# Four-layer recurrent network on one core: head sums of layer 1 go to TensorE, row scalings of the mixer to ScalarE, and the order of all steps is laid out anew

## The reference, cut to what matters

```
# layer 1, for each token: q, k, v are 16 heads of 8
z[h, g]   = sum over d of q[h, d] * k[g, d]          # 16 x 16 scores
w         = entmax15(z)                               # over g
s[h, d]   = sum over g of w[h, g] * v[g, d]
# layer 0, for each chunk: state kept per head
xdt       = x * dt                  # per token and head
xdd       = xdt * decay             # per token and head
state     = state * exp(A_sum) + B^T xdd
```

## Time and profile before

| | us |
|---|---|
| median of 3 runs | 3212.22 (3211.52 to 3215.06) |
| span of the profiled execution, first to last instruction | 3209.0 |
| what lies around the span (median less span) | 3.2 |
| layers 0, 1 and first half of 2, from the span's start | 1945 |
| second half of layer 2 | 288 |
| preparation of layer 3 | 72 |
| attention of layer 3 | 813 |
| feed-forward of layer 3 | 91 |

### The profile page before, as it was taken

How to read it: one execution, slowest core, us unless ns; L and a number is a source line. 1 busy time by engine, 2 the same in 40 slices (tenths; PEclk the granted TensorE clock), 3 DMA queues, 4 the chain that set the end, 5 groups by cost and what they waited for, 6 DMA issues and landing times.

```text
span 3209.0 us, 40003 instructions
## 1 busy us (share of the span) xinstructions
PE 2383.4 (74%) x13729; PEld 1300.2 (41%) x13729; DVE 2544.2 (79%) x5554; ACT 1633.2 (51%) x3182; POOL 565.8 (18%) x610
## 2 busy tenths in 40 slices
PE   3697876967958769679674304997688898888888
PEld 1333333333333333334331101332366676666663
DVE  3386898998999999989989673887577777777764
ACT  1344436245344353353442412666587888777862
POOL 0000300302203003012030020001332323323320
PEclk9698987977978879779777655999799999999999
DMA  2001100100101001001010004200688877888751
GB/s 73 1 22 43 30 25 28 35 32 23 34 29 30 26 24 33 28 27 31 30 24 23 23 8 123 57 9 31 198 226 223 235 222 225 220 215 227 220 157 43
DMA packets 270758, 265.92 MB, mean 83 GB/s; under 512 B 15224, under 2 KB 244235, under 8 KB 268987
## 3 DMA queue, kind: packets, MB, share of 16 engines
q1 hardware_dynamic: 270554, 263.37, 28.8%
HBM read 130.48 MB, written 124.45 MB: 79 GB/s over the span
## 4 chain that ended last, share of the span: by engine, by line
DVE 41%; PE 31%; ACT 14%; issue 9%; DMA 2%; POOL 2%; SPq 1%; DVEq 0%; POOLq 0%; ACTq 0%
PE banks L2642 5%; PE banks L2688 4%; DVE t L2618 3%; DVE t L1017 2%; PE banks L2602 2%; DVE t L1169 2%; ACT L144 2%; DVE t L952 1%; ACT t L2629 1%; PE banks L1085 1%; ACT t L2553 1%; DVE t L2673 1%; DVE t L1700 1%; DVE t L1704 1%; ACT t L1395 1%
## 5 line engine op out<-in xcount | busy, mean ns | idle before, releaser
L2618 DVE CUSTOM_DVE_ANT_0 t<-banks,t 128x640 f32<-128x640 f32 (+7 forms) x512 | 377.8, 747 | 135.2 <-PE banks L2642 62.2
L2629 ACT ACTIVATE t<-t 128x640 f32<-128x640 f32 (+7 forms) x512 | 391.0, 780 | 81.3 <-DVE t L2618 80.4
L2642 PE MATMUL banks<-ident,t 128*128 128x128 f32 x2304 | 360.1, 281 | 41.6 <-DVE t L2839 14.4
L2642 PEld LDWEIGHTS banks<-ident,t 128*128 128x128 f32 x2304 | 253.8, 142 | 108.1 <-ACT t L2629 50.5
L2602 PE MATMUL banks<-t 128*128 128x512 bf16 (+3 forms) x768 | 197.3, 333 | 39.4 <-DVE t L2618 37.5
L2583 POOL TENSOR_TENSOR t<-t 128x512 f32<-128x512 f32 x96 | 122.6, 1277 | 551.1 <-DMA t<-relative_scratch 455.7
L548 POOL TENSOR_TENSOR t<-t 128x512 f32<-128x512 f32 x28 | 48.1, 1718 | 915.7 <-ACT t L520 915.7
L2673 DVE COPY t<-banks 128x512 f32<-128x512 f32 x256 | 175.6, 686 | 32.2 <-PE banks L2642 31.3
L1085 PE MATMUL banks<-t 128*128 128x512 f32 x256 | 145.0, 650 | 42.9 <-DVE t L1165 32.3
L1740 ACT ACTIVATE t<-t 128x16 f32<-128x16 f32 x256 | 82.5, 322 | 184.1 <-DVE t L1704 142.4
L1119 ACT ACTIVATE t<-banks 128x512 f32<-128x512 f32 x128 | 76.4, 597 | 195.6 <-PE banks L1085 195.4
(11 more groups left out here) (453 smaller groups left out, 5956.2 us busy)
## 6 DMA issues: line engine op xcount, KB each, us to landing
relative_scratch<-t SPq DMA_DIRECT2D x128, 512.0 KB, 3.6
t<-relative_scratch SPq DMA_DIRECT2D x128, 512.0 KB, 5.2
relative_scratch<-t SPq DMA_DIRECT2D x128, 256.0 KB, 4.1
t<-in_wmoe SPq DMA_DIRECT2D x64, 384.0 KB, 3.0
t<-cut_scratch SPq DMA_DIRECT2D x192, 64.0 KB
t<-t SPq DMA_DIRECT2D x16, 512.0 KB, 4.2
cut_scratch<-t SPq DMA_DIRECT2D x8, 768.0 KB, 4.1
z_scratch<-t SPq DMA_DIRECT2D x8, 512.0 KB, 3.1
```

What stands on the lines that cost most here:

```text
L2618: nc.vector.tensor_tensor_reduce(s.s[z][:, 0:n], ps[:, b0:b0 + 1 + i // 4, :].rearrange("p b n -> p (b n)")[:, 0:n], s.bias[r][:, j, WIDE ...
L2629: nc.scalar.activation(s.s[z][:, 0:n], s.s[z][:, 0:n], ACT.Exp, scale=-1.0, bias=s.least[:, z:z + 1]).then_inc(*a.mark("weights", u))
L2642: nc.tensor.transpose(ps[:, 4 + c % 2, (t - lo) * P:(t - lo + 1) * P], s.s[u % NS][:, t * P:(t + 1) * P], k.ident[:]).then_inc(*e.mark("tu ...
```

## The change

What it does, part by part:

1. **Scores of att1.** The product (line 952) is laid out as d, h, g in place of h, g, d. The reduction (955) goes; instead TensorE adds the 8 slices of 256 columns into a PSUM bank by 8 matmuls with the identity as weights, and ScalarE copies the sum to `z`.
2. **Output of att1.** The product (1017) is laid out as g, h, d. The reduction (1020) and the transposes (897) go; TensorE adds the 16 slices of 128 columns by 16 matmuls with the slice as weights and the identity as moving data, which also turns the result.
3. **Buffers and banks.** `prod` has two buffers now, the second on the memory of `cum` and `cumsq`. The heads part holds banks 3 and 4 until `z` of the last tile is copied (before: until q, k, v of the last tile are copied).
4. **Mixer.** `xdt`, `xdd` and the scaled state (`kept`, a new buffer) are made by ScalarE, 4 activations with a scale for each row or head; VectorE's lines 599, 611 and 621 go.
5. **Table loads** are issued ahead of the wait of their step in place of behind it.
6. **Order.** All strings `TURNS_*`, `TURNS3_*` and `TURNS4_*` are new.
7. The weights of layer 1 are laid out to match (k by d, v by g), and the masks with them.

```diff
 def att1_pe(k, s, u, free):
...
     for t in range(NT):
-        yield
-        for line, *key in free("heads_out", u):
-            pe.wait_ge(line, *key)
-        pe.wait_ge(v, "s_tok", u, t)
-        nc.tensor.transpose(ps[:, bk, t * P:(t + 1) * P], o.s_tok[:, t], k.ident[:]).then_inc(*e.mark("s_tok", u))
+        for d in range(HD):
+            if d % SOME == 0:
+                yield
+                pe.wait_ge(v, "products", u, t)
...
+            mm(bank(ps, bk + (t + 1) % 2, NH * NH), k.ident[:], o.prod[t % 2][:, d * NH * NH:(d + 1) * NH * NH], start=(d == 0),
+               stop=(d == HD - 1)).then_inc(*e.mark("z", u, t))
+    for t in range(NT):
+        for g in range(NH):
+            if g % SOME == 0:
...
+                pe.wait_ge(v, "valued", u, t)
+            mm(ps[:, bk, t * P:(t + 1) * P], o.prod[t % 2][:, g * D:(g + 1) * D], k.ident[:], start=(g == 0), stop=(g == NH - 1)).then_inc(
+                *e.mark("s_T", u, t))
 def att1_act(k, s, u):
...
+    for t in range(NT):
+        yield
+        act.wait_ge(e, "z", u, t)
+        nc.scalar.copy(o.z[:, t], bank(ps, bk + (t + 1) % 2, NH * NH)).then_inc(*a.mark("z", u, t))
 def att1_dve(k, s, u):
...
-        tt(prod.rearrange("p (h g d) -> p h g d", h=NH, g=NH), rep(q, 2, NH), rep(kk, 1, NH), ALU.mult).then_inc(*v.mark())
-        yield
-        dve.wait_ge(v)
-        reduce(o.z[:, t], prod.rearrange("p (x d) -> p x d", d=HD), AX, ALU.add).then_inc(*v.mark())
+        if t >= 2:
+            dve.wait_ge(e, "z", u, t - 2)
...
+        tt(o.prod[t % 2].rearrange("p (d h g) -> p d h g", h=NH, g=NH), rep(q, 3, NH), rep(kk, 2, NH), ALU.mult).then_inc(
+            *v.mark("products", u, t))
...
-        tt(prod.rearrange("p (h d g) -> p h d g", h=NH, d=HD), rep(w, 2, HD), rep(x, 1, NH), ALU.mult).then_inc(*v.mark())
-        yield
-        dve.wait_ge(v)
-        reduce(o.s_tok[:, t], prod.rearrange("p (x g) -> p x g", g=NH), AX, ALU.add).then_inc(*v.mark("s_tok", u, t))
+        if t >= 2:
+            dve.wait_ge(e, "s_T", u, t - 2)
+        tt(o.prod[t % 2].rearrange("p (g h d) -> p g h d", g=NH, h=NH), rep(w, 3, HD), rep(x, 2, NH), ALU.mult).then_inc(
+            *v.mark("valued", u, t))
 def mixer_act(k, s, u):
...
-        act.wait_ge(v, "xdt", u, t)
+        act.wait_ge(e, "turned", u, t)
         nc.scalar.copy(s.btok[:], ps[:, 0, DI0:DI0 + P]).then_inc(*a.mark("btok", u, t))
+        yield
+        for h in range(H0):
+            nc.scalar.activation(s.xdt[:, h, :], ps[:, 0, h * HP:(h + 1) * HP], ACT.Copy, scale=s.dt[:, t, h:h + 1]).then_inc(
+                *a.mark("xdt", u, t))
...
+        act.wait_ge(a)
+        for h in range(H0):
+            nc.scalar.activation(s.xdd[:, h, :], s.xdt[:, h, :], ACT.Copy, scale=s.dd[:, h:h + 1]).then_inc(*a.mark("xdd", u, t))
+        if u:
+            yield
+            if t:
+                act.wait_ge(v, "state", u, t - 1)
+            for h in range(H0):
+                nc.scalar.activation(s.kept[:, h, :], s.state[:, t, h, :], ACT.Copy, scale=s.ec[:, h, P - 1:P]).then_inc(
+                    *a.mark("kept", u, t))
```

More of the change, by code:

```diff
@@ L513, in mixer_act @@
         yield
+        k.table(LOGEXP)
         act.wait_ge(a)
-        k.table(LOGEXP)
         nc.scalar.activation(s.ec, bank(ps, 2).rearrange("p (h t) -> p h t", h=H0), ACT.Exp).then_inc(*a.mark())
@@ L731, in ffn0_act @@
         yield
+        k.table(SILU)
         act.wait_ge(e, "gate", u, t)
-        k.table(SILU)
         nc.scalar.activation(f.hid[t // 2][:, t % 2], ps[:, S0, 0:FF0], ACT.Silu).then_inc(*a.mark("silu", u, t))
@@ L865, in att1_views @@
     o.qkv = take((NT, 3 * D))
-    o.z, o.cum, o.cumsq = (take((NT, NH * NH)) for _ in range(3))
-    o.s_tok, o.masked = (o.cum.rearrange("p t g -> p (t g)")[:, 0:TB].rearrange("p (t d) -> p t d", t=NT) for _ in range(2))
-    o.prod = take((2 * NT * NH * NH,))
-    o.sa, o.sb = (o.prod[:, i * NT * NH * NH:(i + 1) * NT * NH * NH].rearrange("p (t g) -> p t g", t=NT) for i in range(2))
+    o.z, sums = take((NT, NH * NH)), take((2 * NT * NH * NH,))
+    o.cum, o.cumsq = (sums[:, i * NT * NH * NH:(i + 1) * NT * NH * NH].rearrange("p (t g) -> p t g", t=NT) for i in range(2))
+    o.masked = o.cum.rearrange("p t g -> p (t g)")[:, 0:TB].rearrange("p (t d) -> p t d", t=NT)
+    o.prod = [take((2 * NT * NH * NH,)), sums[:, 0:2 * NT * NH * NH]]
+    o.sa, o.sb = (o.prod[0][:, i * NT * NH * NH:(i + 1) * NT * NH * NH].rearrange("p (t g) -> p t g", t=NT) for i in range(2))
     o.one, o.star, o.tau = take((NT * NH,)), take((NT * NH,)), o.sb
     return o
+SOME = 4
 def att1_pe(k, s, u, free):
@@ L1896, in final @@
 def final(k, name, u):
-    return {"ffn0": (k.line("ffn0_act"), "gate", u), "heads": (k.line("att1_act"), "qkv", u, NT - 1),
+    return {"ffn0": (k.line("ffn0_act"), "gate", u), "heads": (k.line("att1_act"), "z", u, NT - 1),
             "heads_out": (k.line("att1_act"), "s_T", u), "in2": (k.line("in2_act"), "copied", u, NT - 1),
@@ L2153, in readout2_act @@
     yield
+    k.table(ROOT)
     act.wait_ge(e, "var", b)
-    k.table(ROOT)
     nc.scalar.activation(s.stat[:, 0], ps[:, 1, 0:2], ACT.Sqrt, bias=k.eps5[:]).then_inc(*a.mark("root", b))
@@ L2274, in moe2_act @@
     yield
+    k.table(SIGMOID)
     act.wait_ge(e, "logits", b)
-    k.table(SIGMOID)
     nc.scalar.activation(o.rb.score, ps[:, bb, 0:NT * E2].rearrange("p (t e) -> p t e", t=NT), ACT.Sigmoid).then_inc(
@@ L2742 @@
+    "svvstststsvvtsststsvsvtststsvvttssstvstvsststsvvtstsstvsvtsststsvvtsststsvvstststsvvtsststssvvtststvsvttssstsstv"
+    "svtstvsvtstsstsstvstvststvvssttvvvv"
 )
```

304 lines of the change are left out of this document (151 added, 153 removed).

## The result

The changed kernel takes **3208.58 us** (median of 15 runs, 3195.41 to 3215.14) against 3214.45 us of the kernel before on the same chip (15 runs, 3209.22 to 3233.25). The ratio is 0.9964, with an interval from 0.9951 to 0.9977: times 3214, faster by 12 us (7 to 16). The two medians alone lie 6 us apart; wherever a gain is given here, it is worked out from the ratio. The forecast was 158 us. The sign was right, and so was nearly every count of work; the size was not.

What follows compares the result with a forecast made beforehand. VectorE was taken to bound the first stage: 172 us off it less 28 lost gives 144, plus 8 for loads and 6 for later order makes 158, so 3054 us against 3212.22. Range 2995 to 3095 us, chance 0.62.

Steps and rivals of the forecast that it cites:

- The step that failed: First stage: work taken from VectorE shortens the 215.1 us period almost one for one, by 21.5 to 193.6 us.
- Off VectorE: First stage: two reductions a tile (140.8 us) and lines 599, 611, 621 (10.9, 10.9, 9.5) leave VectorE, 172 us.
- the wait for GpSimd: Line 611, mixer: its wait of 1.07 us in 28 cases (30 us) was counted as staying, on the next product.
- The new layout of the two large products: Products of 2048 elements on VectorE: new order costed at nothing, bounds nothing and 22 us.
- TensorE: First stage: sums add 27 us a unit at 2.4 GHz, some 54 at 1.2 GHz; 166 us if the clock is granted.
- ScalarE: First stage: activations, copies and table loads bring it to 113 us a unit, below the period, no term in the sum.
- Table loads: ScalarE: 49 more loads, 127 up to the stage's end; hiding them ahead of waits gives 8 us, between nothing and 45.
- Later stages: After the first stage: the new order of steps gives 6 us, bounds -20 and +30.
- Bank 3 and TensorE take over in part: First stage: rival where the chain of banks 3 and 4 sets about 205 us, gain 80 us, 3132 us; chance 0.17.
- The slower rival: First stage: rival where the hand-over of bank 3 sets the period, 222 us, 56 us more, 3268 us; chance 0.04.
- the signs listed for a wrong forecast: VectorE idle over 25 us a period, TensorE's clock still 0.83, or later stages shorter or longer by over 20 us.

Runs made afterwards that it cites:

- e1: Kernel before, both reductions of layer 1's attention (L955, L1020) reading only the first addend of each sum: 3173.77 us against 3213.48, ratio 0.9887.
- e12: Changed kernel with the old order of the steps after the first stage: 3221.67 us against 3216.85 of the kernel before, ratio 1.0016.
- e2: Kernel before with only the changed order of the later stages (six strings): 3203.93 us against 3213.48, ratio 0.9969.
- e14: Kernel before, both reductions cut to their first addend and the mixer's row scalings on ScalarE, old order: 3193.19 us against 3211.81, ratio 0.994.
- e13: Changed kernel with one sum matmul in place of each group of 8 or 16: 3190.57 us against 3211.81 of the kernel before, ratio 0.9937.
- e3: Kernel before with only the mixer's row scalings moved to ScalarE, in the old order: 3254.23 us against 3213.48, ratio 1.013.
- e8: Changed kernel with the mixer's row scalings put back on VectorE, changed order: 3225.72 us against 3216.49 of the kernel before, ratio 1.0034.
- e7: Kernel before with only ScalarE's table loads moved ahead of their step's waits: 3212.34 us against 3216.49, ratio 0.9987.
- e11: Kernel before with the changed order of the later stages and table loads ahead of their waits: 3188.04 us against 3216.85, ratio 0.9911.
- e10: Changed kernel with each of TensorE's sum matmuls issued twice: 3399.02 us against 3216.85 of the kernel before, ratio 1.0569.
- e6: Kernel before with only the reduction of the output's products (L1020) cut to its first addend: 3208.57 us, ratio 0.9975.
- e5: Kernel before with only the reduction of the scores' products (L955) cut to its first addend: 3205.3 us against 3216.49, ratio 0.9975.
- e15: Changed kernel with one matmul per sum and the mixer's row scalings back on VectorE: 3217.15 us against 3211.81 of the kernel before, ratio 1.002.

## Why the prediction was wrong

**The step that failed** is the one on which the whole sum stood: "Work taken from VectorE here should shorten the period almost one for one", and so "215.1 - 21.5 = 193.6 us". The runs show 36 us back for 115 removed, with nothing added elsewhere (e1). Two readings led to it. A busy share of 94% was taken for a bound. And small waits were taken to confirm it: "with a bank chain as the bound they would have to be far larger". They need not be. Each queue takes the steps of several parts in a fixed order, laid out so that another part's work stands where one part waits; the waits are small *because* the fillers are there, and e1's 2.15 us in the place of 0.23 is one of them uncovered. The chain of waits tells filler from load, and it gave 15 to 21 us of the 53 of each reduction.

That the sign was right owes nothing to this step. Without the later stages' order, a term priced at 6 us, the changed kernel isn't faster than before (e12).

The account of the change, in us against before. Each step is the difference of two ratios, the second and third rows within some 7 and 11 us, the fourth within 9. Runs in the changed order hold the later stages' order too, which is worth 17 us between e12 and the changed kernel (10 in e2) and is taken out of them with 17. The steps lead from one kernel to the next, so that they add up to the measured change by construction; the sum is no test of them.

| step | us | from |
|---|---|---|
| reductions off VectorE, nothing in their place | -36 | e1 |
| scalings to ScalarE, old order | +17 | e14 (-19) less e1 |
| changed order of the first stage, its loads and copies, the longer hold of banks 3 and 4 | +16 | e13 (-20, corrected -3) less e14 |
| sums on TensorE | +9 | changed kernel (-12) less e13 |
| order of the later stages | -17 | changed kernel less e12 (+5) |
| sum | -11 | measured -12 |

**Term by term.** *Off VectorE*: 151 us of busy time in the first stage instead of 172. The 172 already counts the wait for GpSimd as staying, so the missing 21 us are something more. (Line 611 was long in 25 of its 32 cases, not in 28; the waiting in question is 27 us, not 30.) Products that stayed slowed down; before and then after:

```profile
L610 DVE TENSOR_TENSOR t<-t 128x512 f32<-128x512 f32 x32 | 22.1, 690 | 20.3 <-ACT t L520 19.7
L808 DVE TENSOR_TENSOR t<-t 128x512 f32<-128x512 f32 x80 | 54.5, 681 | 0.0
L1700 DVE TENSOR_TENSOR t<-t 128x64 f32<-128x64 f32 x256 | 65.9, 258 | 7.4
```
```profile
L622 DVE TENSOR_TENSOR t<-t 128x512 f32<-128x512 f32 x32 | 26.1, 816 | 21.6 <-ACT t L524 21.6
L817 DVE TENSOR_TENSOR t<-t 128x512 f32<-128x512 f32 x80 | 60.5, 756 | 0.0
L1730 DVE TENSOR_TENSOR t<-t 128x64 f32<-128x64 f32 x256 | 72.2, 282 | 7.3
```

These three lines took 16 us. Only the third has to do with line 611. e3, which moves the scalings alone in the old order, shows where its wait went:

```profile
L620 DVE TENSOR_TENSOR t<-t 128x512 f32<-128x512 f32 x32 | 22.1, 691 | 20.6 <-ACT t L523 19.9
L1708 DVE TENSOR_TENSOR t<-t 128x64 f32<-128x64 f32 x256 | 72.2, 282 | 7.4
L1702 DVE TENSOR_TENSOR t<-t 128x68 f32<-128x68 f32 x256 | 64.8, 253 | 7.3
```

L1702 took 58.2 us before (as L1694), L1683 34.6 in place of 29.1 (as L1675): together 18 us of the 27 came back on products right behind line 610's counterpart, which in 17 of 32 cases took about 1.05 us more than usual. So the prediction was right to count most of the wait as staying. The rule of the Trainium skill ("SBUF — State Buffer", Who interferes with whom) that it cited agrees with that: the waiting moved to other products of two tiles. The slowing of L610 and L808, 10 of the missing 21 us, is not this: e3 has them at 691 and 684 ns, and e8, with line 611 back in the changed order, at 875 and 746. It came with the changed order. The new layout of the two large products cost 3 us more (152.3 in place of 149.3), near the lower end of its bounds. *TensorE*: 18 us of busy time a period more, against 27 at full clock; the sums took 240.8 us of records for 768 matmuls (30 a unit), close to the 28 forecast, and the rest got some 11 us a period shorter while the clock rose from 0.83 to 0.90. *ScalarE*: 113 us a period, as forecast. *Table loads*: exactly 127 up to the end of the stage and 143 in all:

```profile
L144 ACT ACT_TABLE_LOAD x143 | 183.5, 1283 | 5.6 <-DVE centre L174 3.1
```

The idle time before them fell from 62.0 us to 5.6, but in e7, where it fell as far, the time didn't change by anything measurable: 8 us was put on it, and at most 11 are inside e7's interval. Beside the later order the moved loads are worth more: e11 is 19 us (10 to 27) faster than e2. *Later stages*: 6 us with bounds from -20 to +30; 10 (e2) and 17 us (e12) measured, and 29 with the loads moved and the old first stage.

**The rivals.** "Bank 3 and TensorE take over in part" named an engine that did take over, but left 80 us of gain; e10 shows that TensorE's additions count. in the kernel before, a cut inside bank 3's hold (e6) gave no more than one outside (e5); whether its longer hold costs anything in the changed kernel was not tested. The slower rival had half of the idea (a chain sets the pace, so the change's additions count and most of its savings don't) and was dismissed by the misread waits; but no run shows that this chain is the hand-over of bank 3, and it can be compressed: e1 made the period 4 us shorter. Of the signs listed for a wrong forecast, VectorE's idle over 25 us a period is the one that came: 32 us. Of this the waits for the sums (L985 on L914, L816 on L940 in the list above) are 4 us a period.

**What stays open.** With the sums all but gone, the changed kernel still takes 216 us a period with VectorE at 186 and TensorE at 165 us. e15 shows that neither the scalings nor a full engine hold it. That the order does is what is left by elimination, together with the longer hold of banks 3 and 4, and which step it is stays open. Nor was the change's TensorE part tried in the old order.

## What to carry to other kernels

In a kernel whose queues interleave several parts in a fixed order, don't price a saving by the engine's busy share or by how small its waits are: look up, instruction by instruction, how much of it stands on the chain of waits, take that as the upper end, and expect a cut of one thing alone to meet the next chain soon. Before work is moved to another engine, cut it short in place: that costs one line of code and shows the most that a move could bring. A new order of steps, with the waits that come with it, is a change of its own: e15's six periods take 58 us more than e1's at nearly the same work. It has to be measured alone; here the order of the later stages and earlier table loads gave 29 us where the change as a whole gave 12.

## What the hardware did that was not expected

TensorE's busy time grew by less than the work that was added. TensorE runs at 1.2 or 2.4 GHz, and the granted clock is its mean over a stretch, as a share of the latter. Over six periods it rose from 0.83 before to 0.90 with the change's 96 short matmuls a unit, and to 0.92 with each of them doubled (e10); with one of each group (e13) it was 0.84. The mixer's row matmuls (L444), the same in number in both kernels, took, before and then after:

```profile
L444 PE MATMUL banks<-t 128*128 128x128 f32 x256 | 46.6, 343 | 0.0
```
```profile
L444 PE MATMUL banks<-t 128*128 128x128 f32 x256 | 35.7, 285 | 0.0
```

11 us less for the same work, though the trace's records of some matmuls may be missing (the means, 343 and 285 ns, don't depend on that). The order has a part in it too: e13, with nearly all sums left out, has 306 ns there. So in these runs leaving TensorE work out took less off its busy time than the work's own (in e13 17 us a period less, for sums that take some 28).
